# Row maxima of windowed attention moved a quarter of a step, and placed by one transfer

## What is computed

```python
q = rope(einsum(xn, Wq) + bq) * SCALE; k = rope(einsum(xn, Wk) + bk) * SCALE; v = einsum(xn, Wv) + bv
scores = where(abs(i - j) <= 128, q @ k.T, -1e9)
probs = softmax(concat([scores, sinks]))
s = einsum(probs[..., :-1] @ v, Wo) + bo
x = x + s * silu(fp8(xn) @ w_ffn.T + b_ffn)
```

## Time and profile before

| what | value |
|---|---|
| median of 3 runs | 2062.67 us (2051.56 to 2083.64) |
| the profiled execution, its own time | 2063.17 us |
| its span, first to last instruction | 2061.5 us |
| PE, DVE, POOL, ACT busy | 1802.8, 1302.0, 1013.4, 720.8 us |
| mean granted clock of PE | 0.91 |
| steps 0 to 61, from score to score | 1897.3 us |

### The profile page before, as it was taken

The page is one execution under the profiler, slowest core; times in us unless marked ns, Lnnn a source line. Parts: engine busy times, 40 slices in busy tenths (PEclk is TensorE's granted clock), DMA queues, the critical chain, the costliest instruction groups (busy, mean ns, idle before and its releaser), DMA issues.

```text
span 2061.5 us, 34158 instructions
## 1 busy us (share of the span) xinstructions
PE 1802.8 (87%) x11139; PEld 1587.9 (77%) x11139; DVE 1302.0 (63%) x4157; ACT 720.8 (35%) x1509; POOL 1013.4 (49%) x1019
## 2 busy tenths in 40 slices
PE   2379898989989899998989899898998989899888
PEld 1268888877878788887878788887887878788777
DVE  7757665666756665676656666566566666656554
ACT  2124342333433343333333334333333333333332
POOL 3335554554654555465455545356455545535531
PEclk8579898999999898999989989899999999999988
DMA  4534343453344344434425433434433443443430
GB/s 145 131 60 66 69 70 64 82 87 62 65 80 81 62 73 78 73 64 89 70 47 98 75 60 64 83 75 76 76 61 74 75 78 61 74 70 56 90 60 22
DMA packets 81728, 151.95 MB, mean 74 GB/s; under 512 B 13712, under 2 KB 30864, under 8 KB 77456
## 3 DMA queue, kind: packets, MB, share of 16 engines
q1 hardware_dynamic: 81552, 149.76, 39.4%
HBM read 18.64 MB, written 4.19 MB: 11 GB/s over the span
## 4 chain that ended last, share of the span: by engine, by line
PE 64%; DVE 14%; issue 9%; SPq 3%; DMA 2%; POOL 2%; ACT 2%; DVEq 0%; POOLq 0%
PE pv_bank L1143 20%; PE ring L1104 11%; PE ring L1051 8%; PE acc L1166 8%; PE score L1127 5%; PE score L1129 5%; DVE junk L859 4%; DVE neg_parts L874 3%; PE ring L1153 3%; PE ring L1060 2%; SPq L369 2%; DVE neg_max L870 2%; DMA kT_low<-k_second 2%; POOL k_first L525 1%; POOL k_second L527 1%
## 5 line engine op out<-in xcount | busy, mean ns | idle before, releaser
L859 DVE CUSTOM_DVE_ANT_0 junk<-ring,mask 128x384 bf16<-128x384 f32 (+1 forms) x1024 | 488.2, 484 | 564.3 <-PE ring L1104 551.4
L1143 PEld LDWEIGHTS pv_bank<-v,stage 128*128 128x128 f32 x5120 | 738.7, 206 | 26.1 <-issue 11.1
L1143 PE MATMUL pv_bank<-v,stage 128*128 128x65 f32 x5120 | 739.6, 279 | 1.0 <-ACT stage L624 0.5
L547 POOL TENSOR_SCALAR_AFFINE_SELECT stage<-stage 128x512 f32<-128x512 f32 x384 | 241.5, 643 | 807.3 <-ACT stage L624 807.1
L1104 PE MATMUL ring<-kT_high,qT_full 128*128 128x384 f32 (+1 forms) x1024 | 414.5, 406 | 155.1 <-DMA kT_low<-k_second 64.4
L624 ACT ACTIVATE stage<-score 128x512 f32<-128x512 f32 x640 | 356.7, 595 | 438.7 <-PE score L1129 438.1
L1104 PEld LDWEIGHTS ring<-kT_high,qT_full 128*128 128x128 f32 x1024 | 212.6, 208 | 212.3 <-issue 101.5
L665 ACT ACTIVATE oT_hi<-ring 128x256 fp32r<-128x256 f32 x256 | 98.1, 383 | 537.7 <-PE ring L1153 537.7
L1127 PE MATMUL score<-qT_full,kT_high 128*128 128x512 f32 x640 | 280.7, 439 | 5.6 <-ACT stage L624 5.5
L1129 PE MATMUL score<-qT_high,kT_low 72*128 72x512 f32 x640 | 268.4, 419 | 0.0
L897 DVE TENSOR_TENSOR oT_lo<-ring,oT_hi 128x256 fp32r<-128x256 f32 x256 | 108.1, 422 | 112.7 <-ACT oT_hi L665 111.2
(11 more groups left out here) (119 smaller groups left out, 2696.2 us busy)
## 6 DMA issues: line engine op xcount, KB each, us to landing
qT_high<-qT_full SPq DMA_DIRECT2D x64, 512.0 KB, 4.2
qT_full<-q_first SPq DMA_DIRECT2D x64, 256.0 KB, 4.2
qT_full<-q_first_hi SPq DMA_DIRECT2D x64, 256.0 KB, 5.6
qT_full<-q_second SPq DMA_DIRECT2D x64, 256.0 KB, 6.9
qT_full<-q_second_hi SPq DMA_DIRECT2D x64, 256.0 KB, 8.0
kT_high<-k_first_hi SPq DMA_DIRECT2D x128, 64.0 KB, 2.1
kT_high<-k_second_hi SPq DMA_DIRECT2D x128, 64.0 KB, 2.1
qT_high<-turned_rows SPq DMA_DIRECT2D x512, 2.0 KB
```

The lines of the kernel that those rows point to most:

```text
L547: nc.gpsimd.affine_select(out=pr, in_=pr, compare_op=ALU.is_ge, fill=0.0, base=0, pattern=[[0, GROUP], [sign, P]], channel_multiplier=-sign) \
L859: nc.vector.tensor_tensor_reduce(junk[:, h % 2, 0:cols], ring[h % 2][:, 0:cols], mask[:, m0:m0 + cols], 1.0, LOWEST, ALU.add, ALU.max, row ...
L1143: last = nc.tensor.matmul(pv[:, h, :], prob[:, q % 2 * 3 + n, h * P:(h + 1) * P], v[:, slot, k, :], start=(n == 0), stop=(n == len(BLOCKS[ ...
```

## The change

Each tile's score rows and maxima move one slot later: slot `q` of step `it` now handles tile `q - 1` of step `it + 1`, and slot 0 handles tile 3 of `it` itself (`back(it + 1, q, 1)`). Pair 0 is negated, turned and copied in slot 3, pair 1 in slot 1 of the next step. The parts of the maxima are kept as four high rows and four low rows, so that one transfer writes two rows of `qT_high` for all heads, and the second product reads 66 rows, not 72; the zeros are no longer needed. In SyncE's list `keys_in` stands ahead of `rows_in`: before pair 1's rows where the four heads aren't new, and between the two pairs' rows where they are. The second projection of keys for k = 5 moves to slot 1 of k = 6; sums, rounding and low parts of keys move to slots 0, 1 and 2 of k = 2, and to slots 2, 2 and 3 of k = 6. The ffn moves to slots 0 and 2 of k = 1, and two turnings of x move by one slot.

```diff
-    return (0, 1, 2, 3) if q == 0 else (0, 2, 1, 3)
+    return (0, 1, 2, 3) if q == TILES - 1 else (0, 2, 1, 3)
...
         return ("k", 2 * n + 1, q - 2) if 0 <= n < BATCH else None
-    if (k, q) in ((5, 2), (5, 3)):
-        return ("k", 2 * n + 2, q - 2) if n + 1 < BATCH else None
+    if (k, q) in ((5, 3), (6, 1)):
+        return ("k", 2 * n + 2, k - 5) if 0 <= n and n + 1 < BATCH else None
...
         return ("v", n, TILES - 1) if 0 <= n < BATCH else None
-    if (k, q) == (0, 3):
+    if (k, q) == (0, 2):
         return ("xq", n, 1) if 0 <= n < BATCH else None
-    if (k, q) == (5, 1):
+    if (k, q) == (5, 2):
...
                 sp.wait_ge(s_max_rows_done, 2 * s + pair + 1)
-                if s == 0 and pair == 0:
-                    sp.wait_ge(s_ones_ready, 3)
-                for h in range(GROUP):
-                    sp.dma_start(qT_high[D + 2 * h:D + 2 * h + 2, s % 2, h, pair * 2 * P:(pair + 1) * 2 * P]
-                                 .bitcast(F32), turned_rows[2 * h:2 * h + 2, :]).then_inc(s_rows_in, 16)
+                sp.dma_start(qT_high[D:D + 2, s % 2, :, pair * 2 * P:(pair + 1) * 2 * P].bitcast(F32),
+                             turned_rows[:, :]).then_inc(s_rows_in, 16)
...
                     highs_in(b)
+                if real(t) and t % QUAD:
+                    keys_in(t)
...
                     rows_in(it, 1)
-                if real(t) and t % QUAD:
-                    keys_in(t)
...
                     result(n - 1, 0)
+                if real(t) and t % QUAD == 0:
+                    keys_in(t)
...
                     queries_in(a)
-                if real(t) and t % QUAD == 0:
-                    keys_in(t)
...
                         turn_odd(a)
+                    if q == 3 and k == 6 and new_keys:
+                        keys_low(quad)
...
                         second_low(a)
-                    if q == 2 and new_keys:
+                    if (k, q) in ((2, 0), (6, 2)) and new_keys:
                         keys_sum(quad)
-                    if q == 3 and new_keys:
+                    if (k, q) == (2, 2) and new_keys:
...
                         exps(it, q, 2)
-                    if q == 0 and real(it):
+                    if q == 1 and real(it):
                         max_rows(it, 1)
-                    if q == 2 and real(b):
+                    if q == 3 and real(b):
...
                         second_high(a)
-                    if q == 3 and k in (2, 6) and quad < BATCH * QUADS:
+                    if (k, q) in ((2, 1), (6, 2)) and quad < BATCH * QUADS:
...
                 dve.wait_ge(s_small_self, i + 1)
-                parts = neg_parts[:, pair, :, :].rearrange("p t (h w) -> p t h w", w=2)
-                nc.vector.tensor_copy(parts[:, :, :, 0], neg_max[:, :, :]).then_inc(s_mh_done, 1)
+                parts = neg_parts[:, pair, :, :].rearrange("p t (w h) -> p t w h", w=2)
+                nc.vector.tensor_copy(parts[:, :, 0, :], neg_max[:, :, :]).then_inc(s_mh_done, 1)
...
                 dve.wait_ge(s_mh_done, i + 1)
-                nc.vector.tensor_tensor(parts[:, :, :, 1], neg_max[:, :, :], parts[:, :, :, 0].bitcast(F32),
+                nc.vector.tensor_tensor(parts[:, :, 1, :], neg_max[:, :, :], parts[:, :, 0, :].bitcast(F32),
...
                     normalise(n + BATCH, x_in, (k - 2, k - 1))
-                if (k, q) in ((1, 1), (1, 3)) and n < BATCH:
+                if (k, q) in ((1, 0), (1, 2)) and n < BATCH:
...
                     other = chunk_at(n, k, q)
-                    if q == 0 and real(it):
+                    r, tile = back(it + 1, q, 1)
+                    if q == 1 and real(it):
                         negated(it, 1)
-                    if q == 2 and real(b):
+                    if q == 3 and real(b):
                         negated(b, 0)
-                    if real(b):
-                        maximum(b, q, 0)
+                    if real(r):
+                        maximum(r, tile, 0)
...
                 if h == 1:
-                    other = chunk_at(it // KV, it % KV, q)
-                    if q == 0 and real(it + 2):
+                    other = chunk_at(it // KV, it % KV, slot)
+                    if slot == 0 and real(it + 2):
...
                 if h < 2:
-                    upto(pe, s_max_done, done - (0 if h == 1 else 1 if q == 1 else 2))
+                    upto(pe, s_max_done, done - (0 if h == 1 else 1 if q == 0 else 2))
...
                 if n == 0 and q % 2 == 0:
-                    pe.wait_ge(s_rows_in, 16 * GROUP * (2 * c + q // 2 + 1))
+                    pe.wait_ge(s_rows_in, 16 * (2 * c + q // 2 + 1))
...
                                  qT_full[:, c % 2, :, q * P:(q + 1) * P], start=True, stop=False)
-                nc.tensor.matmul(score[blk % 2][:, :], kT_low[0:D + NR, c % 3, k * P:(k + 1) * P],
-                                 qT_high[0:D + NR, c % 2, :, q * P:(q + 1) * P], start=False, stop=True) \
+                nc.tensor.matmul(score[blk % 2][:, :], kT_low[0:D + 2, c % 3, k * P:(k + 1) * P],
+                                 qT_high[0:D + 2, c % 2, :, q * P:(q + 1) * P], start=False, stop=True) \
...
                     c1, c2, c3 = back(it, q, 1), back(it, q, 2), back(it, q, 3)
+                    r, tile = back(it + 1, q, 1)
...
                     def row(h):
-                        if real(b):
-                            score_rows(b, q, h, it)
+                        if real(r):
+                            score_rows(r, tile, h, it, q)
...
                     def maxima_turn():
-                        if q == 0 and real(it):
+                        if q == 1 and real(it):
...
                             turn_max(it, 1)
-                        if q == 2 and real(b):
+                        if q == 3 and real(b):
...
                         if real(c2[0]):
-                            if q == 0 and real(it):
+                            if q == 1 and real(it):
                                 pe.wait_ge(s_max_rows_done, 2 * it + 2)
-                            if q == 2 and real(b):
+                            if q == 3 and real(b):
...
                                 pe.wait_ge(s_xqT_done, KT * n + 1)
-                            if (k, q) in ((1, 1), (1, 3)) and n < BATCH:
+                            if (k, q) in ((1, 0), (1, 2)) and n < BATCH:
...
                         weighed(0)
-                        maxima_turn()
+                        extra()
```

23 lines of the change are left out of this document (13 added, 10 removed).

## The result

| kernel | median | ratio to before, 95% interval |
|---|---|---|
| before | 2067.15 us (2051.56 to 2083.64) | |
| after | 2094.43 us (2088.92 to 2100.16) | 1.0176 (1.0119 to 1.0233) |

The change costs 1.8%, where 5.9% was forecast. The profiled execution took 2088.92 us around a span of 2087.2.

A forecast was written before the change was run, and what follows sets the result against it. Bound: the 10.4 us chain from q's landing to tile 2's third score pair, with q landing later. Steps sum to 241.0 us a sequence, clock drops add 20: 261 against 244.8, +127, less start and last step +122: 2185 us, range 2000 to 2255.

The forecast's parts named there:

- The step that failed is the clock term: Drops of PE's granted clock after short waits: one in seven of eight steps, at 2.9 us, 20 us a sequence.
- The sum at full clock: Steps k = 0 to 7 without clock drops: 28.4, 30.3, 31.8, 29.5, 28.3, 29.6, 32.2, 30.9, together 241.0 us a sequence.
- the chain from q's landing: From q's landing through GpSimd and ScalarE to tile 2's third score pair: a fixed 10.4 us with no slack left.
- Queries 2.1 us later: End of each step: queries leave 3.2 us after tile 3's first score, not 1.13, so q lands about 6.4 in.
- Third pair at 16.8: PE's third score pair of tile 2 stands 6.4 + 10.4 = 16.8 us into the step, now 12.9 to 14.6.
- Pair 1's turn, 1 to 3 us, hidden: Slot 1, beside GpSimd's work: 1 to 3 us of wait for turning, hidden by the bound of 16.8.
- k = 2: Keys' sums and roundings move ahead of q's second half and tile 2's exponentials: the step takes 31.8 us, from 26.6.
- k = 3, k = 6, k = 7: Steps with or behind new keys, whose work delays rows or queries: 29.5, 32.2 and about 30.9 us.
- that the delay isn't felt (1984): Faster rival: PE comes later to tile 2 itself or rows leave sooner; 79 us less, 1984; faster by over 2%: 0.17.
- The rival with the rows of pair 1: Slower in another place: pair 1's rows queue behind six key transfers, tile 2's first score waits; 2124 us, no separate chance.
- the no-change rival, 2065: Two key stops with their clock, 14 us a sequence, matched by about 16 of new waits; 2065 us, chance 0.13.
- if the drops stay at four a sequence: Lower bound with clock drops as now: 241 + 12 = 253 us a sequence, +65, 2128 us.

The follow-up runs named there:

- both sets of keys last: The changed kernel with k = 2's keys handled as before, and new keys of k = 2 and k = 6 sent behind the queries: 2040.22 us, ratio to before 0.986.
- the sink's argument last: The changed kernel, but DVE computes the sink's argument after the two parts of the maxima instead of between them: 2104.28 us, ratio to before 1.023.
- The kernel with q_second and the turn both later: Against both sets of keys last: q_second rounded behind tile 2's first exponentials, and pair 1 turned behind more TensorE work: 2035.4 us, ratio to before 0.988.
- q_second rounded later: Against both sets of keys last: ScalarE rounds q_second after tile 2's first two exponentials instead of ahead of them: 2020.35 us, ratio to before 0.981.
- the rows sent by ScalarE: The changed kernel, but ScalarE, not SyncE, issues the transfer of the maxima's rows, right behind its own copy: 2073.97 us, ratio to before 1.011.
- The kernel with four transfers: The changed kernel with four transfers of the maxima's rows, one a head, in place of one: 2384.77 us, ratio to before 1.162.
- the last experiments: Against both sets of keys last: q_second rounded later (2020.35 us), pair 1 turned later (2052.96), both (2035.4); the k = 4 steps shown are from both.
- the base: The changed kernel with k = 2's keys handled as before and both sets of new keys sent behind the queries: 2040.22 us, ratio to before 0.986.

## Why the prediction was wrong in its size

**The step that failed is the clock term**: "one drop in seven of eight, at 2.9: 20", laid in full on top of steps whose other chains already covered much of it. The sum at full clock was 241.0 a sequence and the mean sequence is 247.6, which leaves 6.6 for the clock. The sum itself was a little high: the shortest step of each k that has the common work adds up to 28.2 + 30.1 + 31.0 + 27.7 + 27.5 + 29.4 + 31.5 + 32.1 = 237.5, and then the term is 10. (Five of these eight still have 3.4 to 6.8 us of low clock, all ahead of the third pair. That this adds little is seen in two other kernels: without any, k = 3 takes 27.5 with both sets of keys last, and k = 5 and k = 7 take 29.8 and 32.2 with the sink's argument last.) Either way the term is about half of 20 or less. The forecast for the steps was +127, the trace has +21.5. Of the 13.4 a sequence between 261 and 247.6, 3.5 lie in the sum (k = 3 alone has 1.8) and 10 in the clock, 28 and 78 us. The start went the other way, 4.5 lost where I had some us of gain (in the kernels run here the first score stands anywhere from 103.9 to 114.5, so chance may be in it), and so the whole is +26 against +122.

Not the number of drops was wrong. I had 7 in 8 steps, the trace has low clock in 48 of 62, 6.2 in 8. Wrong was the price. I took 2.9 from steps k = 4 and k = 6 of the kernel before, where the low stretch lies behind the third pair (27 steps in all have such a stretch), in matmuls that nothing else hides. The change's own stop, TensorE's for turning at 8 to 10 us, puts most drops ahead of the third pair, in the time in which the chain from q's landing runs anyway. I had added the drop to a bound that already held much of it. An estimate from the table of low clock: at a granted clock of 0.50 a stretch loses half its length where nothing covers it. The 93 us behind the third pair are then 46 lost; the 258 us ahead of it would be 129, but with 10 a sequence, 78 us in all, only 32 are left for them, a quarter. Stretches of the changed kernel show the prices one by one: k = 1, which has no such bound, with the low clock ahead of the third pair, then k = 6 with it there and without any, and the first scores behind these two k = 6.

```profile
395.04:427.23 32.19, 29.92 (x194) 26.63 (x193) 20.47 (x70) 10.55 (x22) 14.88 (x16) 0.95 0.37 71
1043.70:1075.20 31.50, 27.21 (x172) 23.50 (x170) 21.14 (x62) 13.07 (x26) 19.89 (x18) 0.95 0.26 48
1545.10:1576.67 31.57, 25.97 (x172) 22.31 (x170) 21.24 (x62) 12.96 (x26) 19.69 (x18) 1.00 0.25 48
```

```profile
1075.18 0.47 PE L1126 MATMUL score<-qT_full,kT_high 128*128 128x512 f32 x1 [1.31 <-issue]
...
1576.67 0.47 PE L1126 MATMUL score<-qT_full,kT_high 128*128 128x512 f32 x1 [2.97 <-issue]
```

k = 1 takes 32.2 with one short drop and 30.2 without: 2.0. k = 6 takes 31.5 with and 31.6 without: nothing, since the step ends in a wait for k = 7's first score, and that wait is 1.3 us behind a drop and 3.0 without one. In k = 3, 4 and 5 the first 3.4 us ahead show little, but a stretch of 6.8 makes the step 1.1 to 1.3 longer than one of 3.4 (27.7 to 29.0, 27.6 to 28.7, 29.8 to 31.0). k = 4 takes 27.5 at 0.94 with a short drop ahead, and 32.6 at 0.79 where it goes on behind the third pair: 5. The kernel with q_second and the turn both later gives the last point from the other side, within one trace: with less to cover it, a drop of 13.7 us takes a step k = 4 from 26.4 to 32.7.

Point by point:

- *Queries 2.1 us later*: right. They leave 3.3 after tile 3's first score (3.2 forecast), q is there at 5.9 to 6.2 (6.4).
- *Third pair at 16.8*: right as a time (means 16.7 to 17.7 in k = 0, 3, 4, 5, 6), wrong in its cause. Bound by the chain, TensorE would wait there for ScalarE for over 100 us; it waits 15.4. It is late by itself, by the stop for turning and the clock behind it, and both end at the same time. Taking away only the chain's end (q_second rounded later) changed little. What moves it is taking away both: with the rows sent by ScalarE q lands earlier and the stop is nearly gone, and it stands at 14.2 in k = 4, not 17.1, and the step takes 27.8, not 30.4.
- *Pair 1's turn, 1 to 3 us, hidden*: right for the size, 0.7 to 2.4 a step in means, 77.3 in all; only partly hidden, as halving it gave about 1 us in k = 3 to 5. The Trainium skill (SBUF — State Buffer, Who interferes with whom) says that a DVE instruction with two SBUF inputs contends with a GpSimd one that reads SBUF. The trace agrees in kind: operations of 8 columns end with three GpSimd products, in a chain of 3.2, not my estimate of 5, and the sum of 2223 did not come. But of the four operations that I counted the cast has one input, and takes 1.20 all the same, and the sink's argument has two and takes 0.15.
- *k = 2*: 31.8 forecast, 34.3 measured; at 31.0 in the one step where no low clock came behind the third pair. There TensorE does wait for ScalarE as foretold (0.9 to 2.1 us), and a drop behind that point does cost.
- *k = 3, k = 6, k = 7*: 29.5, 32.2, 30.9 forecast, 29.6, 31.5, 32.6 measured. A stop of up to 3.0 us stands at the start of k = 7 (10.7 in seven waits); the profile names no releaser, and by their place behind the keys it is put down to the rows of pair 0, as foretold.
- *Rivals*: that the delay isn't felt (1984) fell: steps k = 4 grew. The rival with the rows of pair 1 is real: in the step shown the rows' packets end 1.5 after their issue, at 994.2, and tile 2's first score starts at 994.70. The kernel with four transfers shows it decide; in the changed kernel it has at most 6.3 us in all, 3.6 of them in one step. The measured 2094 lies between the no-change rival, 2065, and the forecast's lower bound "if the drops stay at four a sequence", 2128.

What stays open: why a stop brings the clock down for 3.4 us in one step, for 13.7 in another of the same k and not at all in a third (the k = 4 steps of the last experiments, two of them with nearly the same stops). No run here tells this apart. Nor does any run remove the drops and keep the rest, so the price of a drop rests on steps of the same k with and without one.

## What to carry to other kernels

Before you add the price of a clock drop to a step, look where in the step it will fall: under another chain's bound it costs nothing or a part, behind the last thing that waits it costs all of it, and a price read from drops of one kind says nothing of the other. When a transfer moves in a queue, ask in both directions: what it now delays, and what it protected or was protected from (small rows ahead of a megabyte of queries). When a change bundles several moves, undo each alone: here the later maxima were sound with one transfer, and the keys' move ahead of q lost more than they gained.

## What the runs showed of the hardware

- A transfer of 8 KB issued 1.4 us after the first of four transfers of 256 KB, from another engine's queue, has its packets end 5 to 6 us after its issue in most steps; with nothing ahead of it they end after 1.5. A separate queue did not let it pass.
- DVE operations of 8 columns take 0.17 us by themselves and 0.73 to 1.20 beside GpSimd products of 1.27, each ending with one of them, so that three in a row took 3.2 us; a fourth, between two products, took 0.15. With the products elsewhere the means of the two that make the parts fall from 584 and 506 ns to 219 and 218, and DVE's busy time over the steps from 1203.7 to 1104.5.
- In the changed kernel all 32 steps k = 2 to 5, in which TensorE stands 1.5 to 2.4 us at the turn in means, have the clock's lower level, and of the eight k = 0, with 0.9, only the first. The stretches are mostly 3.4 or 6.8 us long. Cutting the stops (66.0 to 26.2 us) left 36 of 62 steps with low clock, where the base had 44.
